# Weight chunks and cached keys of a paged attention stage: low parts and one cast moved to GpSimd, a ring of eight chunks instead of four

## The reference

```
q = rope(rmsnorm(x @ Wq.T)); k = rope(rmsnorm(x @ Wk.T)); v = x @ Wv.T     # 32 q heads, 8 kv heads, D = 128
kc, vc = k_cache[block_table], v_cache[block_table]                         # 16 pages of 32 keys a sample
k_all, v_all = concat(kc, k), concat(vc, v)                                 # 512 + 128 keys
scores = q @ k_all.T / sqrt(D), masked where a cached key lies past the length
out = x + (softmax(scores) @ v_all).reshape(...) @ Wo.T
```

## Time and profile before

| | |
|---|---|
| time, median of 3 runs | 1526.07 us (1526.06 to 1526.41) |
| profiled execution, own time | 1528.81 us |
| its span | 1527.2 us |
| mean granted TensorE clock | 0.968 of full |
| TensorE busy | 1402.6 us (92%) |
| DVE busy | 1135.4 us (74%) |
| ACT busy | 881.4 us (58%) |
| GpSimd (POOL) busy | 500.6 us (33%) |

### The profile page before, as it was taken

How to read it: one execution, slowest core, us unless ns; L and a number is a source line. 1 busy time by engine, 2 the same in 40 slices (tenths; PEclk the granted TensorE clock), 3 DMA queues, 4 the chain that set the end, 5 groups by cost and what they waited for, 6 DMA issues and landing times.

```text
span 1527.2 us, 26725 instructions
## 1 busy us (share of the span) xinstructions
PE 1402.6 (92%) x7308; PEld 1176.6 (77%) x7308; DVE 1135.4 (74%) x2995; ACT 881.4 (58%) x2001; POOL 500.6 (33%) x626
## 2 busy tenths in 40 slices
PE   6999999738999998879999988899999789999996
PEld 5888888526888887768888877688888667888885
DVE  5532347647888888778888887788888787888885
ACT  5532333236566666756666666566666566666564
POOL 4000000033334444223444433244444243443331
PEclk9999999968999999999999999999999899999999
DMA  8111210563222233232222332222223332323211
GB/s 296 43 57 61 83 42 5 166 226 88 57 55 55 55 96 91 82 90 55 55 62 65 93 101 78 70 56 68 67 59 94 98 102 52 65 59 75 58 28 15
DMA packets 127316, 119.32 MB, mean 78 GB/s; under 512 B 84128, under 2 KB 94752, under 8 KB 127008
## 3 DMA queue, kind: packets, MB, share of 16 engines
q0 software_dynamic: 19936, 57.69, 14.6%
q1 hardware_dynamic: 106608, 60.51, 14.1%
q10 hardware_dynamic: 720, 0.54, 0.1%
HBM read 101.90 MB, written 16.78 MB: 78 GB/s over the span
## 4 chain that ended last, share of the span: by engine, by line
PE 24%; issue 20%; ACT 19%; DVE 10%; SPq 4%; DMA 1%; DVEq 1%; ACTq 0%; POOL 0%; POOLq 0%
PE tail L1419 12%; PE tail L1338 9%; ACT bank L1475 5%; SPq L1249 4%; ACT prT L1485 3%; DVE prT L1632 3%; ACT pr L1501 3%; PE bank L1320 2%; ACT pr L1493 2%; DVE pr L1674 2%; ACT kT L1520 1%; ACT qT L1481 1%; ACT prT L1526 1%; DVE mx L1653 1%; DMA k_raw<-k_pages 1%
## 5 line engine op out<-in xcount | busy, mean ns | idle before, releaser
L1493 ACT ACTIVATE pr<-pr,nm,q_scale 128x640 f32<-128x640 f32 x256 | 235.8, 922 | 123.6 <-DVE nm L1657 112.9
L1338 PE MATMUL tail<-prT,vt 128*128 128x512 f32 x960 | 264.5, 413 | 28.2 <-DVE prT L1632 28.2
L1148 POOL TENSOR_TENSOR tick<-tick 128x1 f32<-128x1 f32 x191 | 45.0, 235 | 669.0 <-PE wide L1368 435.1
L1338 PEld LDWEIGHTS tail<-prT,vt 128*128 128x128 f32 x960 | 174.0, 193 | 80.4 <-DVE prT L1632 48.7
L1653 DVE CUSTOM_DVE_ANT_0 pr<-wide,bias 128x640 f32<-128x640 f32 x256 | 209.8, 820 | 16.0 <-issue 15.9
L1632 DVE TENSOR_TENSOR prT<-wide,prT 128x1024 fp32r<-128x1024 f32 x128 | 153.8, 1222 | 83.0 <-ACT prT L1485 79.0
L1297 PE MATMUL bank<-wqT,xTb 128*128 128x512 f32 x768 | 206.2, 399 | 2.7 <-ACT bank L1475 2.7
L1419 PE MATMUL tail<-woT,oT 128*128 128x512 f32 x768 | 195.9, 398 | 0.0
L1368 PE MATMUL wide<-kT,qT 128*128 128x320 f32 x512 | 166.0, 324 | 23.6 <-DVE mx L1653 21.3
L1368 PE MATMUL wide<-kT_low,qT 128*128 128x320 f32 x512 | 160.1, 313 | 0.0
L1419 PEld LDWEIGHTS tail<-woT,oT 128*128 128x128 f32 x768 | 139.5, 188 | 26.6
(11 more groups left out here) (237 smaller groups left out, 2623.4 us busy)
## 6 DMA issues: line engine op xcount, KB each, us to landing
w_ring<-pair_weights SPq DMA_DIRECT2D x80, 256.0 KB
xTb<-x_transposed POOLq DMA_DIRECT2D x32, 512.0 KB, 3.8
k_raw<-k_pages SPq DMA_DIRECT2D x512, 32.0 KB, 1.8
rope<-rope_tables POOLq DMA_DIRECT2D x32, 256.0 KB
out<-y POOLq DMA_DIRECT2D x32, 256.0 KB, 4.1
w_raw<-w_gate_up SPq DMA_DIRECT2D x10, 512.0 KB
x_transposed<-xh SPq DMA_DIRECT2D x8, 512.0 KB, 6.6
w_raw<-w_down SPq DMA_DIRECT2D x11, 256.0 KB, 2.8
```

Source lines behind the costliest of these rows:

```text
L1338: last = nc.tensor.matmul(tail[g][:, :], vt[:, v_part, j, g * D:(g + 1) * D], prT[:, p_part, j, :], start=(j == 0 and v_part + p_part == 0 ...
L1493: ac.activation(pr[:, h, :], pr[:, h, :], ACT.Exp, bias=nm[:, h:h + 1], scale=q_scale[:, 0, head(h)], accum_out=den[:, h:h + 1]).then_inc( ...
```

## The change

It does five things. GpSimd, not ACT, casts the cached keys. GpSimd, not DVE, makes the low parts of the weight chunks, except chunks 0 to 11 of the first pair; it does so in three groups (0 to 7 and 8 to 11 in turn "next", 12 to 15 and 16 to 19 in turn "out"), the first after the second rotation of DVE, the second after the values. The ring holds eight chunks, and ACT makes the first eight high parts of "next" (the first four of "out") between its copies of rotated queries and keys. SP sends the next keys ahead of the last chunks. TensorE waits for each chunk of a projection by itself. DVE again normalises the first six heads in "next", and TensorE spreads the projections ahead in "next" over heads 2 to 7.

```diff
@@ -41,7 +41,7 @@
 ROUND = 1.5 * 2.0 ** 23
-NRING = 4
+NRING = 8
 NCHUNK = 3 * KT + HP
@@ -1089,11 +1089,29 @@
-def chunks(extra, h):
+def uses(slot):
+    return len(range(slot, NCHUNK, NRING))
+def loaded(pair, i):
+    return pair * (16 * uses(i % NRING)) + 16 * (i // NRING + 1)
+def room(pair, i):
+    return chunks_done(pair, i - NRING + 1) if i >= NRING else chunks_done(pair - 1, i + NRING * (uses(i) - 1) + 1)
+EARLY = {"next": ((0, 1, 2, 3), (4, 5), (6,), (7,)), "out": ((), (12, 13), (14,), (15,)), None: ((), (), (), ())}
+def late(extra, h):
     if extra == "next":
-        return [i for i in range(3 * KT) if i * HP // (3 * KT) == h]
-    return [3 * KT + h] if extra == "out" else []
+        return [h + KT] if h >= KT else []
+    return [h + 14] if extra == "out" and 2 <= h < 6 else []
+def chunk_pair(pair, extra):
+    return pair + 1 if extra == "next" else pair
@@ -1176,14 +1194,24 @@
-        def split_cached(pair, b, n, then_x, shared=True):
+        def low_weights(pair, first, end):
+            for i in range(first, end):
+                pool.wait_ge(s_whi, chunks_done(pair, i + 1))
+                nc.gpsimd.tensor_tensor(weight_place(i, 1), w_ring[:, i % NRING, :], weight_place(i, 0), ALU.subtract).then_inc(s_wlo, 1)
+        def split_cached(pair, b, n, then_x, shared=True, extra=None):
...
+            pool.wait_ge(s_k, u * (16 * NPP) + 16 * NPP)
+            pool.wait_ge(s_sfull, u * HP + HP)
+            carry(n)
+            cached = kT[:, :, 0:L].rearrange("p g (j s) -> p j g s", s=PSIZE)
+            nc.gpsimd.tensor_copy(cached, k_raw[:, :, :, :]).then_inc(s_khi, 1)
             pool.wait_ge(s_khi, u + 1)
-            carry(n)
-            nc.gpsimd.tensor_tensor(kT_low[:, :, 0:L].rearrange("p g (j s) -> p j g s", s=PSIZE), k_raw[:, :, :, :],
-                                    kT[:, :, 0:L].rearrange("p g (j s) -> p j g s", s=PSIZE), ALU.subtract).then_inc(s_klo, 1)
+            nc.gpsimd.tensor_tensor(kT_low[:, :, 0:L].rearrange("p g (j s) -> p j g s", s=PSIZE), k_raw[:, :, :, :], cached,
+                                    ALU.subtract).then_inc(s_klo, 1)
             if then_x is not None:
@@ -1194,6 +1222,9 @@
             nc.gpsimd.tensor_tensor(tick[:, 3:4], tick[:, 1:2], tick[:, 1:2], ALU.add).then_inc(s_yfree, 1)
+            if extra:
+                pool.wait_ge(s_rope, u * G + 2 + FIRST)
+                low_weights(chunk_pair(pair, extra), *((0, 2 * KT) if extra == "next" else (3 * KT, 4 * KT)))
             pool.wait_ge(s_vnew, u + 1)
@@ -1201,20 +1232,22 @@
             nc.gpsimd.tensor_tensor(vt[:, 1, :, :], v_raw[:, :, :], vt[:, 0, :, :], ALU.subtract).then_inc(s_vs, 1)
-        def turn(pair, b, n, share, then_x):
+            if extra:
+                low_weights(chunk_pair(pair, extra), *((2 * KT, 3 * KT) if extra == "next" else (4 * KT, NCHUNK)))
+        def turn(pair, b, n, share, then_x, extra=None):
...
                 n = n + 1
-            split_cached(pair, b, n + 2, then_x, share is not None)
+            split_cached(pair, b, n + 2, then_x, share is not None, extra)
...
         loads(0, 0, 0)
-        split_cached(0, 0, 2, 1, False)
+        split_cached(0, 0, 2, 1, False, "out")
         turn(0, 1, 5, None, 2)
@@ -1222,9 +1255,9 @@
                 turn(pair, b + 3, pair * NCARRY + b * 6 + (START + 6), b + 1, b + 4)
-            turn(pair, B - 1, pair * NCARRY + (START + 6 * (B - 3)), B - 3, 0)
+            turn(pair, B - 1, pair * NCARRY + (START + 6 * (B - 3)), B - 3, 0, "next")
             m = pair * NCARRY + (START + 6 * (B - 2))
-            turn(pair + 1, 0, m, B - 2, 1)
+            turn(pair + 1, 0, m, B - 2, 1, "out")
             turn(pair + 1, 1, m + 6, B - 1, 2)
@@ -1252,23 +1285,26 @@
             for i in range(first, end):
-                before = chunks_done(pair, i - NRING + 1)
                 if not isinstance(pair, int) or i >= NRING:
-                    sp.wait_ge(s_wlo, before)
+                    sp.wait_ge(s_wlo, room(pair, i))
                 chunk = a["pair_weights"][pair * NCHUNK + i] if isinstance(pair, int) else a["pair_weights"][bass.ds(pair * NCHUNK + i, 1)].rearrange("o p n -> (o p) n")
...
         load_keys(0, 0, 0)
+        load_weights(0, 3 * KT, 4 * KT)
         with sp.Fori(0, NPAIR - 1) as pair:
-            load_weights(pair, 3 * KT, NCHUNK)
-            with sp.Fori(0, B - 1) as b:
-                load_keys(1, pair, b + 1)
-            load_weights(pair + 1, 0, 3 * KT)
-            load_keys(2, pair + 1, 0)
-        load_weights(NPAIR - 1, 3 * KT, NCHUNK)
-        with sp.Fori(0, B - 1) as b:
-            load_keys(3, NPAIR - 1, b + 1)
+            load_keys(1, pair, 1)
+            load_weights(pair, 4 * KT, NCHUNK)
+            with sp.Fori(0, B - 2) as b:
+                load_keys(2, pair, b + 2)
+            load_weights(pair + 1, 0, 2 * KT)
+            load_keys(3, pair + 1, 0)
+            load_weights(pair + 1, 2 * KT, 4 * KT)
+        load_keys(4, NPAIR - 1, 1)
+        load_weights(NPAIR - 1, 4 * KT, NCHUNK)
+        with sp.Fori(0, B - 2) as b:
+            load_keys(5, NPAIR - 1, b + 2)
@@ -1286,14 +1322,16 @@
-            AHEAD_NEXT = [0] * 4 + [NPROD // 3 * i for i in range(1, HP - 3)] + [2 * NPROD]
-            def project(i, w, first=0, count=NPROD):
+            AHEAD_NEXT = [0, 0] + [4 * i for i in range(HP - 1)]
+            def project(i, w, first=0, count=NPROD, ready=None):
...
                     k, (x_part, w_part) = step // 3, PASSES[step % 3]
+                    if ready is not None and step % 3 == 0:
+                        pe.wait_ge(s_wlo, ready + k + 1)
                     last = nc.tensor.matmul(bank[i][:, :], xTb[:, x_part, k, :], w[:, w_part, k, :],
@@ -1309,9 +1347,7 @@
                     count = min(end - first, NPROD - step)
-                    if extra == "next" and step == 0:
-                        pe.wait_ge(s_wlo, chunks_done(pair + 1, (which + 1) * KT))
-                    project(*first_two[which], step, count)
+                    project(*first_two[which], step, count, chunks_done(pair + 1, which * KT) if extra == "next" else None)
                     first += count
@@ -1377,8 +1413,7 @@
                 for part in range(2):
-                    pe.wait_ge(s_wlo, chunks_done(pair, (part + 1) * KT))
-                    project(*first_two[part])
+                    project(*first_two[part], ready=chunks_done(pair, part * KT))
             if back:
@@ -1391,10 +1426,7 @@
             if front:
-                if first_turn:
-                    pe.wait_ge(s_wlo, chunks_done(pair, 3 * KT))
-                project(0, wqT[:, :, :, REP * D:QW])
+                project(0, wqT[:, :, :, REP * D:QW], ready=chunks_done(pair, 2 * KT) if first_turn else None)
             if back:
@@ -1457,7 +1489,7 @@
-            act.wait_ge(s_wl[i % NRING], pair * (16 * NCHUNK // NRING) + 16 * (i // NRING + 1))
+            act.wait_ge(s_wl[i % NRING], loaded(pair, i))
             ac.copy(weight_place(i, 0), w_ring[:, i % NRING, :]).then_inc(s_whi, 1)
@@ -1514,10 +1546,6 @@
                 new_keys_values(n)
-            if front:
-                act.wait_ge(s_k, n * (16 * NPP) + 16 * NPP)
-                ac.copy(kT[:, :, 0:L].rearrange("p g (j s) -> p j g s", s=PSIZE), k_raw[:, :, :, :]).then_inc(s_khi, 1)
             if back:
@@ -1546,9 +1574,20 @@
+                def early(place):
+                    for i in EARLY[extra][place]:
+                        if i == 0:
+                            act.wait_ge(c_full[0], before[0] + 1)
+                            act.wait_ge(c_full[1], before[1] + 1)
+                        high_weights(chunk_pair(pair, extra), i)
+                early(0)
                 high(1, 2, qT[:, 0, :], bank[1][:, :])
+                early(1)
                 high(0, 3 + own, kT[:, :, L:NK], bank[0][:, 0:G * S].rearrange("p (g c) -> p g c", g=G))
+                early(2)
                 high(1, 3, qT[:, 1, :], bank[1][:, :])
+                early(3)
             if back:
@@ -1557,21 +1596,14 @@
                 for h in range(HP):
-                    for i in chunks(extra, h):
-                        if i == KT:
-                            act.wait_ge(c_full[1], before[1] + 1)
-                        high_weights(pair + 1 if extra == "next" else pair, i)
+                    for i in late(extra, h):
+                        high_weights(chunk_pair(pair, extra), i)
                     exponential(h)
-                    if extra == "next" and h >= REP:
-                        normalise(n, h - REP)
-                    if ahead and h == (HP - 1 if extra else REP + 1):
+                    if ahead and h == REP + 1:
                         full0.n = (TURN if back else FRONT)[0]
...
-                if extra == "next":
-                    for h in range(REP, SOON):
-                        normalise(n, h)
@@ -1723,13 +1755,10 @@
                     mask_max(h, lambda: reciprocal(h - 2) if h >= 2 else None)
```

(9 more changed lines are left out.)

## The result

Median **1461.3 us** (1460.0 to 1464.6, 4 runs) against 1526.1 (1525.9 to 1526.4, 4 runs) for the kernel before: ratio 0.958, interval 0.956 to 0.960. The profiled execution took 1464.6 us, its span is 1462.9 at a mean granted clock of 0.98. That is inside the range and 10.5 us above the forecast.

The account below looks back on a forecast made before the run. TensorE bounds steady turns (33.9 of 34.15 us); seven long turns cost 87 us over that. Savings 6.0 + 28.3 + 28.2 + 12.8 = 75.3 us from 1528.8 give 1453.5, less 2.7 for the median: 1450.8 us; range 1437 to 1478.

Parts of the forecast that it names:

- Steady turns: Turns away from head-pair changes: 34.15 us falls to 33.90 as GpSimd takes the key cast, 24 turns save 6.0 us.
- 0.25 us is idle: Steady turn: TensorE works 33.9 of 34.15 us, so only 0.25 us a turn can be gained.
- Turn A: First long turn at each head-pair change, 12 chunks in its loop: 48.75 to 39.3 us, three save 28.3.
- landed about 3 us later: Turn A: rope, issued by GpSimd at +20, lands about 3 us after issue; rotation waits another 1.8 us.
- Turn B: Second long turn at each head-pair change, 8 output chunks in its loop: mean 44.7 to 35.3 us, three save 28.2.
- 0.7 for the lock: Turn B: DVE and GpSimd instructions excluding each other cost 0.7 us, beside 0.7 us for late chunks.
- Start: Before the first steady turns: 2.5 us from the key cast's wait, 10.3 from the first long turn; sum 12.8.
- The lock decides: Rival, chance 0.15: six normalisations each wait a whole GpSimd low part; Turn A 44.8, Turn B 39.3, total 1479 us.
- The clock stays low: Rival, chance 0.12: TensorE's clock stays reduced at head-pair changes, costing 3.5 us each; total 1461 us.
- GpSimd not late: Rival, chance 0.08: rope and value split arrive in time, Turn A 36 us; total 1440 us.
- slower: Rival, chance 0.03: in every steady turn key cast and low part slide onto DVE's rotation and small steps; needs 2.8 us a turn.
- no change: Rival, chance 0.01: keys and chunks wait for something else that takes exactly the old place.

Follow-up runs that it names:

- the run with one part alone: Kernel before, with only the cast of cached keys moved from ACT to GpSimd: 1495.3 us, ratio 0.980.
- the runs with one part undone: Kernel after with the key cast back on ACT: 1475.6 us, 0.968; kernel after with all chunk low parts back on DVE: 1493.5 us, 0.974.
- The run with another order: DVE loop written out, key cast held back, SP issuing b=0 rope, plus value split after four low parts, not eight, against kernel after: 1447.8 us, 0.945.
- The rope run: Kernel after with SP, not GpSimd, issuing every rope load once the rotation before is done: 1464.8 us, ratio 0.955.
- the two fastest kernels: Kernel after, DVE loop written out, key cast held back, SP issuing b=0 rope: 1452.2 us; also value split after four low parts: 1447.8 us.

## Why the prediction was right, and where it was not

**Bound and mechanism.** Right. Steady turns were bound by TensorE, A by DVE's loop, and B by the keys; the key cast and the low parts each did what was said, and the run with one part alone and the runs with one part undone show it. The larger ring, the early high parts and the early keys were not run by themselves. The total is closer than its terms deserve.

**Steady turns, 6.0 against 13.6 us.** The failed step is "0.25 us is idle". It took TensorE's matmul row as the whole wait. The weight loads ahead of it waited 0.88 us. The turn shrank by 0.65, and the bound of "0.3 a turn" in the prediction was no bound. The turns ahead of A gave 0.5 us of it back (34.0 for 33.5; with the key cast alone they are 33.5), which fits the "at most 1 us" for high parts in the gaps.

**Turn A, 28.3 against 24.5.** The second and third A, 38.8 and 38.7, are 0.6 better than the 39.3 of the sum, and its items are in place: low parts of 1.41 us (1.35 forecast), low 8 to 11 done at +17.6 (+18.7), rope issued at +18.6 (+20), waits of 1.4 for rope (1.8) and 2.3 for the value split (1.3). The run with another order shows that this stall was worth 1.4 us. What is missing from the sum is in the first A, 44.3: rope 3.1 us late put the rotation onto the key work. The rope run shows it, 38.1 in place of 44.3. The term that was too small there is "landed about 3 us later": 4.9 us from issue to rotation. No step of the prediction placed the key work of A beside anything.

**Turn B, 28.2 against 14.9: the step that failed.** "Keys of b=1 ... are wanted only at +20 by GpSimd" and rope "in time" were both right, and from them followed "0.7 for the lock". The step asked whether GpSimd's work is late for somebody and did not ask on what DVE runs when it comes. The key low part met the rotation (2.67 for 0.68 us), a normalisation met the value low part (3.23 for 0.54), and DVE's gap of 3.3 us, hidden in the kernel before, came out. With the gap and the collision removed B is 36.6, and with the small instructions free too, by the luck of the phase, 34.3, below the 35.3 of the sum.

**Start, 12.8 against 11.6.** Right in sum, not in its parts. Up to the last copy of the first queries 4.9 us were gained (339.2 for 344.1; forecast 2.5), and the first long turn went from 45.84 to 39.1, not to 35.5: 6.7 for 10.3. It lacks what B lacks: the key work met the rotation (1.97 and 2.62 us for 0.68 and 0.42 at 359.8 and 361.7). SP issued the keys 7 us sooner (316.1 for 323.0), and the key cast alone gave 7 of the 11.6.

**The rivals.** *The lock decides*: half true. It was not six normalisations that waited (in the second B one of them did, 3.23 us, and the others took 0.5 to 0.6), but the rotation; its B of 39.3 was nearly the measured one (39.7 on the mean), its A of 44.8 was met once, by another cause. *The clock stays low*: false but for the first A. Of the six turns, 0.89 to 0.96 before, the second and third A stand at 1.00, the B at 0.96 (one stretch of about 3.4 us each, 933 to 936.5 in the second, at the end of TensorE's wait of 2.15 us); A and B of the two fastest kernels all stand at 1.00. Most of their waits are gone, but a wait of 2.16 us was left in one B with no fall of the clock behind it, where the 2.15 us one here had a fall; what parts the two is not shown. The clock is part of what TensorE's own time lost (39.6 to 35.2 in the second A, at 0.90 and 1.00). *GpSimd not late*, *slower* and *no change*: false.

**The two rules of the Trainium skill.** With the first, the Trainium skill, SBUF — State Buffer, Who interferes with whom, the traces agree: DVE instructions of 0.16 to 0.96 us took up to one GpSimd low part more (2.06, 2.67, 2.98, 3.23 us), those with two SBUF inputs and tensor_scalar alike, the latter down to ten elements a row, and DVE's prT, which reads PSUM and SBUF, took its 1.2 us beside the same key low part in every steady turn. The figure of the Trainium skill, SBUF — State Buffer, SBUF: two separate sides, a DMA issue that grows to about 3100 ns, was the wrong one to weigh: the page gives it for an issue under a DVE `tensor_copy`, and DVE's rotation is made of `tensor_tensor`. Beside the rotation the indirect issues took 0.94 to 1.43 us in all runs, so nothing of the 2.5 us a turn came. The 1.49 us issue that the prediction puts beside a normalisation stood beside a weight low part of DVE (352.62 to 353.30, two SBUF inputs); the normalisation had ended at 352.70.

## What to carry to other kernels

When work moves to GpSimd, write down for each of its instructions which DVE instruction runs at that offset, in every kind of turn; being in time is not enough, and a wait that holds GpSimd back can be worth 2 us in such a turn. An empty place of under 1 us between two such instructions is fragile: single delays of DVE by 1.4 to 2.0 us in steady turns grew to 1.9 and 3.1 us, because they put a normalisation onto the key low part. Read the weight loads' waits beside the matmuls' before calling a wait the whole idle time. A part's worth measured alone is not its worth beside the others (30 or 14 us for one cast), and when two causes lie on one spot the first one removed shows nothing.
